# One core of Trainium2, causal attention and soft mixture of experts: a reordered opening, last attention group and expert stage, and an addition on GpSimd that waits for VectorE's shift

## The reference

```python
q, k, v = (gelu(x @ W1 + b1) @ W2 + b2  for each of q, k, v)
scores = einsum('bid,bjd->bij', q, k) / sqrt(256 * 512)
scores = scores * tril(ones)                       # causal, no softmax
out = einsum('bij,bjd->bid', scores, v)
x = layernorm(x + layernorm(out) * ln_w + ln_b)    # the second without weights
xn = layernorm(x) * gamma + beta
logits = einsum('bnd,des->bnes', unit(xn) * scale, unit(mu))
dispatch = softmax(logits, over the tokens n)
combine = softmax(logits, over all experts and slots)
slot_in = einsum('bnd,bnes->besd', xn, dispatch)
h = gelu(slot_in @ w1 + b1);  slot_out = h @ w2 + b2
out = layernorm(x + einsum('besd,bnes->bnd', slot_out, combine))
```

## Time and profile before

| what | value |
|---|---|
| median of three runs | 585.02 us (585.01 to 585.04) |
| the profiled execution | 584.8 us |
| its span, first to last instruction | 582.7 us |
| mean granted clock of TensorE | 0.995 of full speed |
| PE busy | 565.2 us, 97% of the span |
| DVE busy | 489.7 us, 84% |
| POOL busy | 421.2 us, 72% |
| ACT busy | 406.9 us, 70% |
| DMA | 59.64 MB, 102 GB/s on the mean |

### The profile page before, as it was taken

The page is one execution under the profiler, slowest core; times in us unless marked ns, Lnnn a source line. Parts: engine busy times, 40 slices in busy tenths (PEclk is TensorE's granted clock), DMA queues, the critical chain, the costliest instruction groups (busy, mean ns, idle before and its releaser), DMA issues. The chain is left out here.

```text
span 582.7 us, 12013 instructions
## 1 busy us (share of the span) xinstructions
PE 565.2 (97%) x3892; PEld 525.7 (90%) x3892; DVE 489.7 (84%) x1052; ACT 406.9 (70%) x870; POOL 421.2 (72%) x406
## 2 busy tenths in 40 slices
PE   9999999999999999999999999989999999989992
PEld 7989989999899999999999989979999999978992
DVE  6579889899898889988989889998988777548996
ACT  4765666676767667766667676677679988754884
POOL 0869779798797787977979879785658777453553
PEclk9999999999999999999999999999999999999997
DMA  7424133042240422413304223024776777875965
GB/s 226 92 74 108 20 92 75 36 110 33 76 108 8 100 35 73 108 18 90 74 34 108 31 77 75 9 29 77 153 154 144 145 145 146 141 167 162 323 238 181
DMA packets 166930, 59.64 MB, mean 102 GB/s; under 512 B 139854, under 2 KB 159724, under 8 KB 166892
## 3 DMA queue, kind: packets, MB, share of 16 engines
q1 hardware_dynamic: 166608, 58.89, 43.3%
q10 hardware_dynamic: 284, 0.27, 0.1%
HBM read 27.68 MB, written 14.68 MB: 73 GB/s over the span
## 5 line engine op out<-in xcount | busy, mean ns | idle before, releaser
L529 POOL TENSOR_TENSOR h_lo<-xn_all,h_hi 128x512 fp32r<-128x512 f32 x32 | 41.6, 1301 | 68.0 <-ACT xn_all L645 67.0
L643 ACT ACTIVATE h_hi<-bank,bias_col 128x512 fp32r<-128x512 f32 x96 | 66.5, 692 | 18.7 <-PE bank L800 17.1
L798 PE MATMUL bank<-xnT_hi,w_hi 128*128 128x512 f32 x188 | 76.2, 405 | 0.0
L799 PE MATMUL bank<-xnT_lo,w_hi 128*128 128x512 f32 x188 | 74.4, 396 | 0.0
L800 PE MATMUL bank<-xnT_hi,w_lo 128*128 128x512 f32 x188 | 74.2, 395 | 0.0
L678 ACT CAST state_hi<-bank 128x512 fp32r<-128x512 f32 x57 | 33.6, 589 | 49.1 <-PE bank L933 49.1
L1702 PE MATMUL bank<-xn_all,e_tok 128*128 128x257 f32 x256 | 65.1, 379 | 0.0
L1197 DVE TENSOR_TENSOR state_lo<-bank,state_hi 128x512 fp32r<-128x512 f32 x57 | 39.4, 692 | 29.2 <-ACT state_hi L678 29.2
L1805 DVE STREAM_TRANSPOSE e_turn<-e_tok 128x256 f32<-128x256 f32 x64 | 40.1, 635 | 16.3 <-ACT e_tok L1587 14.8
L1587 ACT ACTIVATE e_tok<-bank,shift,xinv 128x256 f32<-128x256 f32 x64 | 36.2, 566 | 19.1 <-PE bank L1692 12.2
L1702 PEld LDWEIGHTS bank<-xn_all,e_tok 128*128 128x128 f32 x256 | 44.1, 189 | 3.8
(11 more groups left out here) (222 smaller groups left out, 2198.9 us busy)
## 6 DMA issues: line engine op xcount, KB each, us to landing
x_all<-in_L_attn_x SPq DMA_DIRECT2D x16, 512.0 KB, 4.1
kT<-k_turn SPq DMA_DIRECT2D x128, 64.0 KB, 2.5
ET_all<-e_turn SPq DMA_DIRECT2D x64, 128.0 KB, 4.0
xn_all<-in_xT SPq DMA_DIRECT2D x15, 512.0 KB, 4.7
out<-xn_all SPq DMA_DIRECT2D x15, 512.0 KB, 3.8
x_spill<-x_all SPq DMA_DIRECT2D x12, 512.0 KB, 2.9
ET_all<-x_spill SPq DMA_DIRECT2D x8, 512.0 KB, 5.2
w_sb<-in_L_ffn_w SPq DMA_DIRECT2D x2, 512.0 KB, 5.4
```

Source lines behind the costliest of these rows:

```text
L529: pool.tensor_tensor(h_lo[:, V_SLOT, m, :], hv[:, m, :], h_hi[:, V_SLOT, m, :].bitcast(F32), ALU.subtract).then_inc(hv_split, 1)
L643: nc.scalar.activation(h_hi[:, h_slot(j, n), m, :], ps, ACT.Gelu, bias=bias(n, m))
L798: nc.tensor.matmul(ps, w[0], xs[0], start=start, stop=False, skip_group_check=shared)
L799: nc.tensor.matmul(ps, w[0], xs[1], start=False, stop=False, skip_group_check=shared)
```

## The change

Six places are touched; no operation is added but one activation on four columns, and none is taken away.

- **First loads.** The load of W1k goes from the head of SP's queue to the head of ACT's, so that the two halves of xT are SP's first. DVE clears the zeros of the warm-up before v_sum.
- **Opening group (g = 1).** PE does update_state of tile 0, then hidden(WV1, 0), then the rest of chunk 0. POOL's split_vsum(a, 1) goes up behind scale_mu.
- **Last group (g = 15).** DVE's bias_v(0) and bias_v(1) each go up by one statement; two of the sums of v go into last_body, behind the mask and behind tail_state(2), and floor_norms stands before split_xnT. ACT's second pair of norms is parted, and round_vsum(a, 0) goes behind round_state. POOL's invert_o(a, 1) goes behind split_ktok(1), and split_vsum(a, 1) stands before add_beta(1, 1).
- **Last fold.** A new semaphore, half_folded, is signalled by the first of the last tile's two matmuls; DVE divides half 0 when it has come, then half 1.
- **Experts.** ACT computes a Gelu on four columns before copy_slots, and the two round_e stand one before each Gelu instead of both before the first.
- **Mixing.** add_residual(k) waits until shift_y(k - 1) has been signalled.

```diff
-load_weight(WK1, W1k)
 for kb in range(KB):
...
     if not project:
-        add_beta(pool, 1, 1)
         split_vsum(a, 1)
+        add_beta(pool, 1, 1)
         invert_norms(pool, 0, 0, minus_half[:, :])
...
         scale_mu()
+        split_vsum(a, 1)
     split_hv(g, 0)
...
         invert_o(pool, a, 0)
-    if attend:
+    if attend and settle:
         split_vsum(a, 1)
...
     split_ktok(g, 0)
-    if attend:
+    if attend and more:
         invert_o(pool, a, 1)
...
     split_ktok(g, 1)
+    if not more:
+        invert_o(pool, a, 1)
     if more:
...
 rows = ((b1k, WK1), (b1q, WQ1), (b1v, WV1))
+act.dma_start(w_in[:, WK1, :, :], W1k.rearrange("(k p) n -> p k n", p=P)).then_inc(weight_loaded[WK1], 16)
 for b_row, n in rows:
...
         round_state(ba, i + 1, tail_hi[1])
+        round_vsum(a, 0)
         round_xnT(act, 0, 0)
...
     if not more:
-        norms(act, 0, 0, (2, 3))
+        norms(act, 0, 0, (2,))
     round_v(g, 0)
-    round_v(g, 1)
     if not more:
-        round_vsum(g, 0)
+        norms(act, 0, 0, (3,))
+    round_v(g, 1)
     if not attend:
...
-def chunk(a, ja, ba, c, p):
+def chunk(a, ja, ba, c, p, updated=False):
     i = GT * ja + c
-    if i == 0:
+    if i == 0 and not updated:
         update_state(a, c, True)
...
         pe.wait_ge(mu_copied, 1)
-    if attend:
+    if opening:
+        update_state(a, 0, True)
+    elif attend:
         chunk(a, ja, ba, 0, p)
     hidden(g, j, WV1, 0)
+    if opening:
+        chunk(a, ja, ba, 0, p, updated=True)
     if attend:
...
-nc.vector.memset(v_sum[:, 0, :], 0.0)
 nc.vector.memset(zeros, 0.0).then_inc(zeros_set, 1)
+nc.vector.memset(v_sum[:, 0, :], 0.0)
 nc.vector.memset(rs_o[:, :], 0.0).then_inc(z_ready, GT)
...
         follow(3)
+        if not more:
+            bias_v(g, j, 0)
         pair_statistics(dve, a, 1)
...
         floor_mu()
-    bias_v(g, j, 0)
+    if more:
+        bias_v(g, j, 0)
+    else:
+        bias_v(g, j, 1)
     if attend:
...
         weight_out(a, 3)
+    if not more:
+        sum_v(g, j, 0)
+        return
     bias_v(g, j, 1)
     if attend:
-        if not more:
-            sum_v(g, j, 0)
-            sum_v(g, j, 1)
-            return
         add_out(dve, a, 2)
...
     mask_scores(a)
-    sum_v(a, ja, 2)
+    sum_v(a, ja, 1)
     tail_state(2)
+    sum_v(a, ja, 2)
     split_masked(a)
...
     tail_state(3)
-    split_xnT(dve, 0, 0)
     floor_norms(dve, 0, 0)
+    split_xnT(dve, 0, 0)
     dve.wait_ge(v_split, 2 * GROUPS)
...
 tile_folded = msem("tile_folded")
+half_folded = msem("half_folded")
 rinv_ready = msem("rinv_ready")
...
     pool.wait_ge(mix_scaled, k + 1)
+    if k > 0:
+        pool.wait_ge(y_shift, k)
     yk = y[k % GB][:, SUMMED, 0:D]
...
     if last:
+        act.wait_ge(n2_ready, GT * GROUPS + 1)
+        nc.scalar.activation(square[:, 0, 0:4], square[:, 0, 0:4], ACT.Gelu)
         copy_slots(b)
...
 route(B - 1, last=True)
-round_e(GROUPS - GB + 1)
-round_e(GROUPS - GB + 2)
 for half in range(2):
+    round_e(GROUPS - GB + 1 + half)
     act.wait_ge(hs_biased, 2 * half + 2)
...
                                 xn[q][:, t % GT, :], start=(t == 0), stop=(t == TB - 1))
+        if b == B - 1 and t == TB - 1 and s == 0:
+            last.then_inc(half_folded, 1)
     last.then_inc(tile_folded, 1)
...
 def normalise_slots(b):
-    dve.wait_ge(tile_folded, TB * b + 2 * TB)
+    if b < B - 1:
+        dve.wait_ge(tile_folded, TB * b + 2 * TB)
     for s in range(SB):
+        if b == B - 1 and s == 0:
+            dve.wait_ge(half_folded, 1)
+        elif b == B - 1:
+            dve.wait_ge(tile_folded, TB * b + 2 * TB)
         nc.vector.reciprocal(colinv[:, s:s + 1], fold_ps(b)[s][:, D:D + 1]).then_inc(colinv_ready, 1)
-    for s in range(SB):
         dve.wait_ge(colinv_ready, SB * b + s + 1)
```

More of the change, by code:

```diff
@@ L573, in body @@
                     if not project:
+                        split_vsum(a, 1)
                         add_beta(pool, 1, 1)
-                        split_vsum(a, 1)
                         invert_norms(pool, 0, 0, minus_half[:, :])
@@ L1085, in _ @@
             def _(dve):
+                nc.vector.memset(zeros, 0.0).then_inc(zeros_set, 1)
                 nc.vector.memset(v_sum[:, 0, :], 0.0)
-                nc.vector.memset(zeros, 0.0).then_inc(zeros_set, 1)
                 nc.vector.memset(rs_o[:, :], 0.0).then_inc(z_ready, GT)
@@ L1294, in last_body @@
                     mask_scores(a)
+                    sum_v(a, ja, 1)
+                    tail_state(2)
                     sum_v(a, ja, 2)
-                    tail_state(2)
                     split_masked(a)
@@ L1300, in last_body @@
                     tail_state(3)
+                    floor_norms(dve, 0, 0)
                     split_xnT(dve, 0, 0)
-                    floor_norms(dve, 0, 0)
                     dve.wait_ge(v_split, 2 * GROUPS)
```

## The result

The changed kernel takes 586.14 us (median of 18 runs, 584.91 to 586.96) against 584.83 for the kernel before on the same chip (18 runs, 582.71 to 586.25): a ratio of 1.0027 (1.0016 to 1.0038). It is slower by about 0.27%, where 584.3 with a range of 583.0 to 585.4 had been forecast. The profiled execution after took 586.96, the longest of its 18, that before 584.8.

What follows compares the result with a forecast made beforehand. TensorE is busy nearly throughout, so only seams where it waits or another engine ends last count: -0.27 - 0.17 + 0.41 - 0.92 + 0.20 = -0.75, from 585.02 to 584.27. Range, 8 in 10: 583.0 to 585.4.

Steps and rivals of the forecast that it cites:

- Mixing: Mixing loop: the addition's wait slows early rounds to 3.03 but frees the held shifts from group 11; +0.2 in sum.
- The bound of -0.1: Mixing: lower bound of its term, if TensorE's pace hides part of the early loss; the upper bound was +0.5.
- The end of the attention block: Last group: add_beta, now behind the remainder, holds floor_norms, so VectorE ends the block later than TensorE did; +0.41.
- Rival 1: End of the attention block: floor_norms runs beside add_beta, -0.7 instead of +0.41, giving 583.16, faster; chance 0.18.
- The 0.3 that a power beside scale_tokens might have cost: End of the attention block: by the skill's rule a power should hold scale_tokens too, up to 0.3 later.
- The last fold and the experts: Last fold to experts' second stage: half 0 divided earlier, table load in ACT's idle time, bias comes last; -0.92.
- Rival 2: Last fold: the division of half 0 starts no earlier, -0.48 instead of -0.92, time 584.7; chance 0.12.
- The opening: Start of kernel: first loads let the first product start earlier, -0.27; opening group loses TensorE's wait for GpSimd's remainder, -0.17.
- Rival 3: Mixing: the long shift isn't the addition's doing, stays 0.63, and the addition waits behind it; 586.2, slower; chance 0.10.
- The base: Whole kernel: the median before, 585.02, from which the forecast of 584.27 was reckoned.

Runs made afterwards that it cites:

- the memsets: Kernel before with three one-column memsets on GpSimd ahead of mixing's addition, so that the shift is issued first: 583.79 us, ratio 0.9989.
- the seven and the six profiles: Profiles of kernels with the opening's edit (seven) and with the opening of before (six), read at the last group's add_beta: 0.46 apart in the mean.

## Why the prediction was wrong

- **Mixing, the step that failed.** +0.20 was forecast, +1.41 came: the term was mis-sized. I put the period with the wait at 3.03; it is 3.085, mostly since the addition starts 0.13 behind the shift's end and not 0.08. From where I started, the addition of group 14 came 0.95 later than worked out: 0.11 at the start, 9 x 0.055 = 0.50 in the rounds, and 0.34 at a late store, for which the sum had no term; the second late store took the rest. Without late stores the wait costs 0.78, as its run alone shows. The bound of -0.1 did not come true either: I called the pace of 2.85 TensorE's, so that an early loss might partly hide. TensorE does end its groups 2.84 apart in both kernels, but its lag stays at +0.86 while the loop's grows to +2.27, so it does not hold the loop with the wait; and the pace of before is as much VectorE's, whose own seven instructions fill the round with 0.04 idle in all (557.54 to 560.38 in its trace is 2.84). There was no slack, and from group 5 on each round paid 0.24 to 0.25 in full against the 2.85. What I expected of the shifts was right (0.16 in every group), as was that rounds of 3.21 go; but those belong to some runs only.
- **A reading of the earlier trace rows that was wrong**, though the sum did not suffer by it. The shift of 0.16 at 544.50 does not run beside the power, which ended at 544.47, but starts 0.06 ahead of the addition (544.56) and overlaps it. So it is not free because GpSimd does a power; it is the order of issue that decides, as the memsets showed.
- **The clock, a step that was missing.** I worked out that VectorE would end the block at 396.36 - 0.44 = 395.92 (measured 395.93) and that TensorE could end at 394.95 or sooner (393.97), and stopped there. The wait that this leaves to TensorE, 2.48 instead of 0.53, was treated as free, and in most runs it cost 1.2 afterwards.
- **The end of the attention block: right**, in size and in mechanism; floor_norms was held by add_beta, as the earlier trace rows had shown for another instruction. Rival 1 fell with that. (396.36 less 395.93 is 0.43, not the 0.41 of the sum.) The 0.3 that a power beside scale_tokens might have cost did not come: with floor_norms behind split_xnT the two overlap (393.14 and 393.31), and scale_tokens takes 1.66, as in after, where the power has ended before it.
- **The last fold and the experts: right**, -0.91 for -0.92. Rival 2 fell: the bias came 0.43 earlier where 0.44 had been put.
- **The opening: right in its sum** (-0.36 in after's trace, -0.46 between the means of the seven and the six profiles, -0.44 forecast), **wrong in its parts.** The first product came no earlier but later, 5.30 and not the 4.82 that -0.27 would give, because W1k became the load that lands last: I had asked when xT lands, and not when W1k does. What this stage brought on balance is not shown. The sentence of the Trainium skill ("DMA: Bandwidth & Descriptors", section "Issuing engines are not separate DMA queues") by which only issuing time is saved fits the trace: xT was issued 0.51 earlier (0.81 against 1.32) and its cast started 0.16 earlier. The opening group brought 0.29, not 0.17: I had counted the wait and not the 0.11 by which the matmul behind it was longer.
- **Rival 3** gave 586.2, near the time that came, by a mechanism that did not: the shifts did fall to 0.16.
- **The base.** 585.02 was taken as the kernel's one time. It is one of two, some 1.9 apart, and the range of a forecast should have been laid around that.

Left open: the step at 431, where in the profile of after a power on GpSimd is 2.38 long beside scale_tokens (1.18 before), +1.1 of which 0.6 comes back by 461. None of the other twelve profiles has a power of more than 1.19 there, so it may belong to this one execution. Open too is why a store is late in some profiles and not in others.

## What to carry to other kernels

Before a wait is put into a loop, add up the busy time of each engine over one round: if one of them has no gap, the whole wait is paid in each round, and changing the order in which two colliding instructions are issued can do what making one wait for the other's end would pay for. When an edit lets TensorE finish earlier than the engine that ends a stage, ask what its longer idle time does to the clock of the next stage, not only who ends last. And look at the single times of the kernel before, not just the median: two clusters can mean that a trace shows one of two behaviours.

## What the runs showed of the hardware

- A vector instruction of 128x4 took 0.16 when issued 0.04 ahead of GpSimd's addition and 0.63 when issued 0.03 behind it, and a loop in which both wait on each other kept either order until a late store changed it; in the traces, mixing without held shifts was 1.61 shorter than before's, and the two times of before lie 1.9 apart.
- A VectorE instruction of 128x4 on SBUF (floor_norms) took 1.45 when it started 0.76 behind GpSimd's addition of 128x1024, and ended with it; 0.26 when it started 0.24 before the addition's end; 0.16 with none beside it.
- After TensorE had waited 2.48 or 2.50 at the end of a stage in which it was busy nearly throughout, the profiles of two kernels show the granted clock at 0.50 for about three microseconds; by times and mean clocks this came in 13 of 18 runs of one and 4 of 10 of the other. After waits of 1.29 and 1.30 three profiles show 1.00, and one does after 2.48.
- With the load of W1k moved from one queue to another, xT's cast started 0.16 earlier and W1k's at 4.82 instead of 3.63, so that the first product came 0.21 later: what was gained in one load was lost in the other.
